# A hybrid block on one core: meetings inside the transformer calls dropped, first steps of what follows put in the last feed-forward rounds, loops written out, 3 and 3 banks

## The chip, the cores and the metric

One core of a Trainium2 chip runs the whole kernel. Its engines are TensorE (PE in the profile: matrix products and transposes, into eight PSUM banks of 128x512 fp32), VectorE (DVE), ScalarE (ACT), GpSimd (POOL) and SyncE (SP, which here only issues DMAs). Each takes its own instructions in order and waits for the others by semaphores. The metric is the device time of one execution in microseconds. Before the change it was 2386.45 us, the median of three runs (2385.03 to 2386.71).

## The reference

Eight sequences of 512 tokens and 128 features go through four steps, each added to a residual and fed with a layer norm of it:

```
x = x + mamba_block(layernorm(x))      # phase m
x = x + transformer(layernorm(x))      # phase t0, call 0
x = x + decayed_attention(layernorm(x))# phase a
x = x + transformer(layernorm(x))      # phase t1, call 1
```

The transformer has DEPTH = 2 layers. A layer shifts half the features by one token, projects to q, k and v (8 heads of 64), normalises and rotates q and k, attends within windows of 64 tokens and the window before, projects out and adds. Then it shifts again, takes a layer norm, goes up to 2 x 341 features, multiplies one half by the exact gelu of the other, goes down to 128 and adds. The decayed attention has 16 heads of 8 over all 512 tokens; its scores are multiplied by exp(-|rate| x distance) before the softmax.

## The kernel before, in words

The work is cut by sequence (B = 8) and by tile of 128 tokens (TPS = 4 a sequence). X holds the residual and Y the normed input, both in SBUF for the whole run. Every engine has its own written order; there is no planner. `run` (line 1996 and on) goes through the phases m, t0, a, t1 on each engine and ends each with `meet` (line 332 and on): the engine drains, adds one to a semaphore, and waits until all five have done so.

**A transformer call** is `transformer_sp`, `_pe`, `_act`, `_dve` and `_pool`. For each layer l it runs eight rounds of attention, then a meeting, then eight rounds of feed-forward, then, except after the last layer, another meeting. With the meeting at the phase's end a call has four. q counts sequences over layers and calls, s within a layer.

*Attention.* Before the first sequence the engines fill a pipeline: SyncE stages the shifted input in yq (`stage_shifted`, L446 to L450), TensorE transposes it (L513), VectorE copies it to hT (L835), TensorE projects tiles 0 and 1 to q, k (L519) and v (L526), ScalarE squares (L708) and copies v (L714), VectorE rotates (L842, L847) and sums squares (L854, L856), GpSimd adds (L1004), takes the root (L1010) and normalises (L1019). `qk_transpose` (L533) and the projections of tile 2 follow. Then `attention_sequence` does, for each tile, scores (a mask product L546 and products L553), maxima (L860), exponentials (L730), transposes of the probabilities (L566), the products with v (L578), the transposes of the outcome (L586), the output projection (L592) and its addition (L878), with the preparation of later tiles in between. GpSimd builds the rope tables of the layer first (L1040, L1044), after the wait for the attention weights.

*Feed-forward.* SyncE stages the shifted Y of each sequence in one of two buffers fq (`stage_ff`, L459 to L461); it waits for the sequence's last output addition and until the buffer's last user has been normalised. Sequences 0 and 1 are staged before the meeting and 2 to 7 after it, then come the loads of the next attention weights (`load_attn`, L423 to L426). VectorE takes statistics (`ff_stats`, L912, L917), GpSimd the inverse root (`ff_rstd`, L1055, L1057), VectorE normalises (`ff_normalize`, L925). TensorE transposes (`ff_normed`, L626) and ScalarE scales to fnT (L767). In `ff_round`, TensorE goes up in three steps i of two products each (`ff_up`, L638, into banks 3 to 6 by turns), ScalarE takes the gelu of one (L762), VectorE multiplies (`ff_product`, L933), and TensorE goes down for the sequence before (`ff_down`, L647, bank 7 or 0), which VectorE adds (`ff_add`, L943). TensorE's order in a round is up 0, transposes of sequence q+1, up 1, down of q-1, up 2. VectorE's is product 2 of q-1, statistics of q+2, product 0, normalisation of q+2, product 1, addition of q-1. In a last layer GpSimd adds Y to X (`pre_add`, L1049), and in call 0 VectorE and GpSimd also take the layer norm of sequences 0 and 1 for the decayed attention there (`norm_stats`, `norm_rstd`, `norm_apply`).

*Decayed attention.* `x_transpose` (L1141) and `project` (L1149) make q and k, ScalarE adds the bias (`with_bias`, L1268, L1269), GpSimd splits the result in three bf16 parts (`split`, L1390 to L1397), SyncE writes them to DRAM (`send`, L1111) and reads them back in nine combinations, a half of the heads at a time (`combine`, L1107). Then, per head: four score products (L1165) into banks 0 and 1 by turns, VectorE scales them and takes their maxima (L1319), GpSimd subtracts (L1403), TensorE transposes in four turns (`turn`, L1174) into banks 2 to 5, ScalarE takes the exponential (L1276) and TensorE multiplies with v (`weigh`, L1185) into bank 6. Bank 7 serves the projections.

Most of the sequences are rounds of a loop on each engine (`Fori`, a counter in a register and a jump back); the first and the last one or two of a phase are written out.

`credits` gives semaphores a start value, so that a wait for "n uses ago" is a plain wait for a count. For the banks of the decayed attention these are:

```python
(scaled_done, 2), (aexp_done, TPS)
```

## Time and profile before

| | |
|---|---|
| runs (3) | 2386.45 us median, 2385.03 to 2386.71 |
| the profiled execution | 2385.01 us |
| its span, first to last instruction | 2383.2 us |
| instructions in the profile | 60302 |
| TensorE busy | 2184.3 us (92%) |
| VectorE busy | 1627.2 us (68%) |
| ScalarE busy | 1489.7 us (63%) |
| GpSimd busy | 1679.1 us (70%) |
| granted TensorE clock, mean | 0.97 of full speed |
| SyncE's DMA queue | 119248 packets, 82.70 MB |
| the two instruction queues | 69 packets, 1.13 MB and 77 packets, 0.63 MB |

A busy share is the time in which the engine had an instruction under way. It is a mean over stages that have little in common, so the stretches are to be read one by one. The stretches are: mamba phase to about 300 us, then call 0 (attention to 593, feed-forward to 671, attention to 963, feed-forward to 1045), the decayed attention (first scores at 1072) to about 1630, then call 1 (attention to 1931, feed-forward to 2010, attention to 2301, feed-forward to the end).

In the rows, a time in brackets is how long the engine had been idle before, with what ended that wait. "DVEq L336" there is the meeting's wait.

### The profile page before, as it was taken

To read this page: it belongs to the slowest core of one execution; us is meant where nothing else is said; L and a number is where in the kernel's file an instruction comes from. 1 tells how busy PE (TensorE), PEld (TensorE's weight loads), DVE (VectorE), ACT (ScalarE), POOL (GpSimd) and SP (SyncE) were. 2 spreads that over 40 slices of the span, in tenths; PEclk is the share of its full clock that TensorE was granted. 3 is DMA by queue.
4 is the path that set the end of the run, shared out by engine and by line. 5 is a ranking of instruction groups with operands and counts; after the bars stand their busy time and mean duration, and the time that the engine had idled before them with its cause. 6 is when DMAs were issued, how large, how long until landed. Compare 5 with 4: busy or idle time off the path is not lost. (4 is left out here: it accounts for less than half of the span.)

```text
span 2383.2 us, 60302 instructions
## 1 busy us (share of the span) xinstructions
PE 2184.3 (92%) x19744; PEld 1490.5 (63%) x19760; DVE 1627.2 (68%) x3905; ACT 1489.7 (63%) x4130; POOL 1679.1 (70%) x1712
## 2 busy tenths in 40 slices
PE   6998789998989999859999999998999978999979
PEld 4766557776557777535655656564777755677755
DVE  5777578886557777537666667675878745777755
ACT  3556368887358887325655556554888843888853
POOL 5777788886168888228777777766889822888842
PEclk8999899999999999889999999998999999999999
DMA  4000011111111111112111111101111112111101
GB/s 111 1 0 1 6 27 34 40 37 30 48 36 36 36 34 33 27 58 58 54 42 34 52 53 37 49 21 25 28 34 40 43 23 51 36 34 36 39 21 50
DMA packets 121250, 86.69 MB, mean 36 GB/s; under 512 B 85560, under 2 KB 102160, under 8 KB 118800
## 3 DMA queue, kind: packets, MB, share of 16 engines
q1 hardware_dynamic: 119248, 82.70, 14.3%
q10 hardware_dynamic: 1856, 2.23, 0.3%
q8 instruction: 69, 1.13, 0.2%
q14 instruction: 77, 0.63, 0.1%
HBM read 30.38 MB, written 8.39 MB: 16 GB/s over the span
## 5 line engine op out<-in xcount | busy, mean ns | idle before, releaser
L1319 DVE CUSTOM_DVE_ANT_0 store<-bank,store 128x512 f32<-128x512 f32 x512 | 340.1, 689 | 170.2 <-PE bank L1165 108.6
L1403 POOL TENSOR_SCALAR store<-store 128x512 f32<-128x512 f32 x512 | 349.7, 694 | 149.5 <-DVE store L1319 147.4
L1276 ACT ACTIVATE store<-bank 128x512 f32<-128x512 f32 x512 | 287.1, 603 | 251.2 <-PE bank L1174 247.7
L730 ACT ACTIVATE store<-bank,store 128x128 f32<-128x128 f32 x1024 | 364.2, 378 | 68.5 <-DVE store L860 68.4
L1010 POOL TENSOR_TENSOR store<-store 128x16 f32<-128x16 f32 x128 | 372.5, 2910 | 26.6 <-DVE store L856 26.6
L1004 POOL TENSOR_TENSOR store<-store 128x512 f32<-128x512 f32 x256 | 321.0, 1275 | 85.0 <-DVE store L847 83.7
L1174 PEld LDWEIGHTS bank<-store 128*128 128x128 f32 x2048 | 241.4, 142 | 130.4 <-ACT store L1276 74.1
L1174 PE MATMUL bank<-store 128*128 128x128 f32 x2048 | 298.3, 278 | 0.0
L519 PE MATMUL bank<-store 128*128 128x512 f32 x512 | 270.1, 615 | 7.1 <-DVE store L835 6.6
L1019 POOL TENSOR_TENSOR store<-store 128x512 f32<-128x512 f32 x256 | 261.5, 1043 | 17.4 <-POOL store L1010 11.4
L860 DVE TENSOR_REDUCE store<-bank 128x4 f32<-128x512 f32 x256 | 165.0, 686 | 130.4 <-PE bank L553 130.4
L736 ACT ACTIVATE store<-bank 128x512 f32<-128x512 f32 x256 | 157.8, 616 | 114.0 <-PE bank L566 114.0
L730 ACT ACTIVATION_READ_ACCUMULATOR store<-bank,store 128x1 f32 x1024 | 222.1, 217 | 0.0
L1165 PE MATMUL bank<-store 72*128 72x512 bf16 x512 | 183.2, 389 | 39.5 <-DMA store<-parts 22.0
L638 PE MATMUL bank<-store 128*128 128x512 f32 (+1 forms) x384 | 189.4, 630 | 27.8 <-DVE store L933 22.8
L533 PEld LDWEIGHTS bank<-store 128*128 128x128 f32 x1024 | 116.3, 141 | 129.1 <-POOL store L1019 103.2
L533 PE MATMUL bank<-store 128*128 128x128 f32 x1024 | 154.8, 281 | 35.1 <-POOL store L1019 33.1
L842 DVE TENSOR_TENSOR store<-bank,store 128x512 f32<-128x512 f32 x256 | 174.5, 682 | 12.9 <-issue 6.2
L847 DVE TENSOR_TENSOR store<-bank,store 128x512 f32<-128x512 f32 x256 | 174.4, 681 | 0.0
L592 PEld LDWEIGHTS bank<-store 128*128 128x128 f32 x1024 | 133.5, 192 | 63.8 <-ACT store L741 38.7
L762 ACT ACTIVATE store<-bank,store 128x512 f32<-128x512 f32 (+1 forms) x96 | 65.9, 686 | 170.7 <-PE bank L638 168.4
L566 PEld LDWEIGHTS bank<-store 128*128 128x128 f32 x1024 | 120.8, 141 | 75.9 <-issue 68.1
(199 smaller groups left out, 4457.3 us busy)
## 6 DMA issues: line engine op xcount, KB each, us to landing
store<-store SPq DMA_DIRECT2D x256, 128.0 KB, 2.3
store<-parts SPq DMA_DIRECT2D x96, 192.0 KB
parts<-store SPq DMA_DIRECT2D x16, 384.0 KB, 3.6
store<-store SPq DMA_DIRECT2D x128, 32.0 KB
store<-store SPq DMA_DIRECT2D x128, 31.8 KB
store<-store SPq DMA_DIRECT2D x32, 127.0 KB
store<-in_L_ffn_wqkv_dram SPq DMA_DIRECT2D x4, 768.0 KB, 4.6
out_dram<-store SPq DMA_DIRECT2D x8, 256.0 KB, 2.5
```

Source lines behind the costliest of these rows:

```text
L519: nc.tensor.matmul(bank[i][:, :], hT[:, j * P:(j + 1) * P], wqkv[:, i * INNER:(i + 1) * INNER], start=True, stop=True).then_inc(qk_done, 1)
L533: last = nc.tensor.transpose(bank[5 + i][:, b * P:(b + 1) * P], roped[:, i, b * P:(b + 1) * P], ident)
L638: nc.tensor.matmul(to, w1[:, half * HID + at:half * HID + at + n], fnT[:, odd, :], start=True, stop=True).then_inc(up_done, 1)
L730: last = nc.scalar.activation(prob[:, e, b, :], bank[3 + e][:, b * P:(b + 1) * P], ACT.Exp, bias=nmax[:, e, b:b + 1], accum_out=psums[:, h ...
L1004: nc.gpsimd.tensor_tensor(straight[:, at, :], straight[:, at, :], turned[:, at, :], ALU.add).then_inc(add_done, 1)
L1010: nc.gpsimd.tensor_tensor(flat, flat, minus_half[:, 0:2 * H], ALU.pow).then_inc(norm_done, 1)
L1019: nc.gpsimd.tensor_tensor(roped[:, i, :].rearrange("p (h d) -> p h d", d=DH), straight[:, at, :].rearrange("p (h d) -> p h d", d=DH), bc(n ...
L1165: nc.tensor.matmul(bank[t % 2][:, :], QC[0:COMBO, h, t * P:(t + 1) * P], KC[0:COMBO, h, :], start=True, stop=True).then_inc(score_done, 1)
L1174: last = nc.tensor.transpose(bank[2 + c][:, t * P:(t + 1) * P], S[:, h % 4, t, c * P:(c + 1) * P], ident)
L1276: nc.scalar.activation(AT[:, h % 4, c, :], bank[2 + c][:, :], ACT.Exp, scale=-1.0).then_inc(aexp_done, 1)
L1319: nc.vector.tensor_tensor_reduce(out=S[:, h % 4, t, :], in0=bank[t % 2][:, :], in1=decay[:, off:off + L], scale=1.0, scalar=-3.0e38, op0=A ...
L1403: nc.gpsimd.tensor_scalar(s_, s_, -1.0, amax[:, h % 4, t:t + 1], ALU.mult, ALU.add).then_inc(shifted_done, 1)
```

## The change

It has five parts.

1. **The meetings inside a call go.** Only the one at each phase's end stays. Waits on single semaphores take their place: TensorE waits for the last v copy before it transposes for feed-forward in bank 2, for the last exponentials before it goes up into banks 3 and 4, for the last copy of the probabilities before banks 5 and 6, for the last output addition before bank 7 is used, and for all feed-forward additions before the next layer's scores. Feed-forward's transposes and its up steps 0 and 1 of the first sequence are put between the last steps of attention. SyncE stages sequences 2 to 7 right after the last v shifts; the loads of the next attention weights stand behind the staging of sequence 3, and those of the second layer's feed-forward weights inside its attention, before the last staged sequence.
2. **The next layer's fill is put in the last rounds of feed-forward.** The four input transposes (now bank 1) in round 6, the projections of tile 0 in round 7, those of tile 1 around the last down (now bank 3), then the q, k transposes of tile 0 and the projections of tile 2. VectorE, ScalarE and GpSimd have their parts at the matching places.
3. **The decayed attention's first steps are put in call 0's last feed-forward.** Layer norm of sequences 0 and 1 in rounds 3 and 5, transposes and first projection in round 4, second projection in round 5 (all in bank 1), the splits after GpSimd's last pre-addition, sending and combining at the end of SyncE's part of the call.
4. **All loops are written out**, in every phase: `with pe.Fori(1, B - 1) as s` becomes `for s in range(1, B - 1)`.
5. **The decayed attention's banks** are 3 for the scores (0 to 2) and 3 for the turns (3 to 5), by a running count, in place of 2 and 4.

The diff, cut to its core:

```diff
+        SCORE_BANKS, TURN_BANKS = 3, 3
-                   (scaled_done, 2), (aexp_done, TPS), (at_done, 16), (ao_ready, 1), (av_out, TPS),
+                   (scaled_done, SCORE_BANKS), (aexp_done, TURN_BANKS), (at_done, 16), (ao_ready, 1), (av_out, TPS),
...
         def transformer_sp
-                if l:
-                    sp.wait_ge(down_added, q0 - B + 2)
-                    for j in range(TPS):
-                        stage_shifted(sp, 0, q0, j)
-                    meet(sp, 2 * l + meets)
-                    load_ff(sp, l)
-                with sp.Fori(0, B - 1) as s:
+                for s in range(0, B - 1):
                     if l == 0:
                         sp.wait_ge(ln_ready, B * norm + s + 2)
+                    else:
+                        sp.wait_ge(down_added, q0 - B + s + 3)
+                        if s == B - 2:
+                            load_ff(sp, l)
...
-                meet(sp, 2 * l + meets + 1)
                 for s in range(2, B):
                     stage_ff(sp, s, q0 + s)
-                if call == 0 or l == 0:
-                    load_attn(sp, 1 - l)
+                    if s == 3 and (call == 0 or l == 0):
+                        sp.wait_ge(wo_done, 4 * (q0 + B))
+                        sp.wait_ge(tab_ready, 6 * (l + (call * DEPTH + 1)))
+                        load_attn(sp, 1 - l)
+                if l < DEPTH - 1:
+                    sp.wait_ge(down_added, q0 + 2)
+                    for j in range(TPS):
+                        stage_shifted(sp, 0, q0 + B, j)
...
         def transformer_pe
+            def ff_rounds(q0, l):
+                new = l < DEPTH - 1
+                q1 = q0 + B
+                for s in range(B):
+                    q, odd = q0 + s, s % 2
+                    if s:
+                        ff_up(q, 0, odd)
+                    if new and s == B - 1:
+                        pe.wait_ge(attn_w, (l + 1 + (call * DEPTH + 1)) * (16 * ATTN_LOADS))
+                        pe.wait_ge(down_added, q0 + B - 1)
+                        begin_qk(q1, 0)
+                    if call == 0 and not new and s == 4:
+                        decayed_x(pe)
+                    if s < B - 1:
+                        ff_normed(q + 1)
+                    if s:
+                        ff_up(q, 1, odd)
+                    if new and s == B - 2:
+                        begin_x(q1)
+                    if new and s == B - 1:
+                        project_v(q1, 0, False)
+                    if call == 0 and not new and s == 5:
+                        decayed_project(pe, 1)
+                    if s:
+                        ff_down(q - 1, 1 - odd, bank[7 if odd else 0])
+                    ff_up(q, 2, odd)
+                    if call == 0 and not new and s == 4:
+                        decayed_project(pe, 0)
+                if new:
+                    begin_qk(q1, 1)
+                ff_down(q0 + (B - 1), 1, bank[3])
+                if new:
+                    project_v(q1, 1, False)
+                    qk_transpose(q1, 0)
+                    for i in range(2):
+                        project_qk(q1, 2, i)
...
-                with pe.Fori(1, B - 1) as s:
+                for s in range(1, B - 1):
                     attention_sequence(q0 + s, True, True)
                 attention_sequence(q0 + (B - 1), True, False)
+                ff_normed(q0, True)
                 weigh_values(q0 + (B - 1), TPS - 1)
+                pe.wait_ge(ff_w, (l + (call * DEPTH + 1)) * (16 * FF_LOADS))
+                ff_up(q0, 0, 0, True)
                 o_transpose(q0 + (B - 1), TPS - 1)
+                ff_up(q0, 1, 0, True)
                 project_out(q0 + (B - 1), TPS - 1)
-                meet(pe, l * 2 + meets + 1)
...
+                pe.wait_ge(wo_added, 4 * (q0 + B) + 1)
+                ff_rounds(q0, l)
...
         def transformer_act
+                    ff_gate(q, 0, odd)
+                    if new and s == B - 1:
+                        squares(q1, 0)
+                    if call == 0 and not new and s == 4:
+                        decayed_copy_xT(act)
+                    if s < B - 1:
+                        ff_affine(q + 1, 1 - odd)
+                    ff_gate(q, 1, odd)
+                    if new and s == B - 1:
+                        copy_v(q1, 0)
+                    if call == 0 and not new and s == 5:
+                        decayed_with_bias(act, 0)
+                    ff_gate(q, 2, odd)
+                    if call == 0 and not new and s == 5:
+                        decayed_with_bias(act, 1)
...
         def transformer_dve
+                    if s:
+                        ff_product(q - 1, 2, 1 - odd)
+                    if decayed and s == 3:
+                        dve.wait_ge(down_added, q0 + 3)
+                        norm_stats(dve, n, 0, 0, FIRST)
+                    if s < B - 2 and s:
+                        ff_stats(q + 2, odd)
+                    ff_product(q, 0, odd)
+                    if new and s == B - 1:
+                        dve.wait_ge(tab_ready, 6 * (l + 1 + (call * DEPTH + 1)))
+                        rotate_tile(q1, 0)
+                    if s < B - 2:
+                        if s == 0:
+                            ff_stats(q + 2, odd)
+                        ff_normalize(q + 2, odd)
+                    if decayed and s in (3, 5):
+                        norm_apply(dve, n, s // 2 - 1, 4 * (s // 2 - 1))
+                    ff_product(q, 1, odd)
+                    if new and s == B - 1:
+                        square_sums(q1, 0)
+                    if s:
+                        ff_add(s - 1, q - 1, bank[7 if odd else 0], not new)
+                    if new and s == B - 2:
+                        for j in range(TPS):
+                            take_x(q1, j, True)
+                ff_product(q0 + (B - 1), 2, 1)
+                if new:
+                    rotate_tile(q1, 1)
+                    square_sums(q1, 1)
+                ff_add(B - 1, q0 + (B - 1), bank[3], not new)
...
         def transformer_pool
+                if l:
+                    pool.wait_ge(rot_done, 8 * q0 + 2)
                 pool.wait_ge(attn_w, (l + (call * DEPTH + 1)) * (16 * ATTN_LOADS))
                 rope_tables()
...
                 if call == 0 and last_layer:
+                    for t in range(2):
+                        decayed_split(pool, t)
...
         def decayed_pe
-                nc.tensor.matmul(bank[t % 2][:, :], QC[0:COMBO, h, t * P:(t + 1) * P], KC[0:COMBO, h, :],
+                nc.tensor.matmul(bank[(64 * q + k) % SCORE_BANKS][:, :], QC[0:COMBO, h, t * P:(t + 1) * P], KC[0:COMBO, h, :],
...
-            x_transpose(0, True)
-            project(0, 0)
-            project(0, 1)
...
-            with pe.Fori(1, B - 1) as q:
+            for q in range(1, B - 1):
                 sequence(q, True, True)
```

## Rows read from the trace of the kernel before

**Rows 1.** Windows: stretch, us, busy PE, PEld, DVE, ACT, POOL; clock, DMA

```profile
593.00:671.00 78.00, 70.40 (x320) 42.80 (x320) 37.29 (x108) 28.43 (x37) 7.59 (x12) 0.96 0.16 38
...
1045.00:1072.00 27.00, 2.87 (x9) 0.97 (x10) 0.48 (x1) 4.41 (x6) 6.62 (x7) 0.65 0.28 82
...
1072.00:1630.00 558.00, 540.28 (x3912) 331.71 (x3912) 386.31 (x1197) 321.82 (x586) 413.32 (x583) 0.99 0.16 43
```

**Rows 2.** Timeline, SyncE, first feed-forward: start us, us, line, operation

```profile
594.62 6.52 SPq L461 DMA_DIRECT2D store<-store  x1
...
635.47 6.53 SPq L461 DMA_DIRECT2D store<-store  x1
```

**Rows 3.** Timeline, VectorE, first statistics after the meeting

```profile
603.26 0.87 DVE L912 BATCH_NORM_STATS2 store<-store 128x6 f32<-128x128 f32 x4 [8.27 <-DMA store<-store]
```

**Rows 4.** Timeline, TensorE, first feed-forward and the next layer's start

```profile
587.90 1.44 PE L578 MATMUL bank<-store 128*64 128x64 f32 x32
...
591.48 1.16 PE L592 MATMUL bank<-store 128*128 128x128 f32 x8 [0.69 <-ACT store L741]
...
610.54 0.60 PE L626 MATMUL bank<-store 128*128 128x128 f32 x4
...
651.88 0.60 PE L626 MATMUL bank<-store 128*128 128x128 f32 x4
...
652.31 1.88 PE L638 MATMUL bank<-store 128*128 128x512 f32 x4
...
654.03 2.84 PE L647 MATMUL bank<-store 128*128 128x128 f32 x24
...
656.71 5.31 PE L638 MATMUL bank<-store 128*85 128x512 f32 x12
...
687.95 0.41 PE L546 MATMUL bank<-store 64*64 64x512 bf16 x4
```

**Rows 5.** Timeline, TensorE and SyncE, from call 0 to the decayed attention

```profile
1041.13 2.92 PE L647 MATMUL bank<-store 128*128 128x128 f32 x24 [1.00 <-DVE store L933]
...
1071.93 1.03 PE L1165 MATMUL bank<-store 72*128 72x512 bf16 x2 [22.03 <-DMA store<-parts]
...
1052.14 0.39 SPq L1111 DMA_DIRECT2D parts<-store  x1
```

**Rows 6.** Timeline, VectorE and TensorE, decayed attention, starts of sequences

```profile
1276.63 0.69 DVE L1319 CUSTOM_DVE_ANT_0 store<-bank,store 128x512 f32<-128x512 f32 x1 [2.56 <-PE bank L1174]
...
1346.86 0.69 DVE L1319 CUSTOM_DVE_ANT_0 store<-bank,store 128x512 f32<-128x512 f32 x1 [2.75 <-PE bank L1174]
...
1486.16 0.69 DVE L1319 CUSTOM_DVE_ANT_0 store<-bank,store 128x512 f32<-128x512 f32 x1
...
1553.81 0.69 DVE L1319 CUSTOM_DVE_ANT_0 store<-bank,store 128x512 f32<-128x512 f32 x1
...
1277.39 0.39 PE L1165 MATMUL bank<-store 72*128 72x512 bf16 x1 [1.56 <-DVE store L1319]
```

**Rows 7.** Timeline, TensorE, the same two places in the second layer

```profile
960.67 1.90 PE L592 MATMUL bank<-store 128*128 128x128 f32 x8 [0.69 <-ACT store L741]
...
982.13 0.60 PE L626 MATMUL bank<-store 128*128 128x128 f32 x4
```

**Rows 8.** Timeline, VectorE, a normalisation in the last feed-forward

```profile
2354.58 3.99 DVE L925 TENSOR_SCALAR store<-store 128x128 f32<-128x128 f32 x4 [0.90 <-POOL store L1057]
```

**Rows 9.** Timeline, GpSimd, root and normalisation, written out and in the loop

```profile
555.61 2.91 POOL L1010 TENSOR_TENSOR store<-store 128x16 f32<-128x16 f32 x1 [0.21 <-DVE store L856]
...
558.60 2.04 POOL L1019 TENSOR_TENSOR store<-store 128x512 f32<-128x512 f32 x2
...
2084.30 2.91 POOL L1010 TENSOR_TENSOR store<-store 128x16 f32<-128x16 f32 x1 [0.21 <-DVE store L856]
...
2087.43 2.04 POOL L1019 TENSOR_TENSOR store<-store 128x512 f32<-128x512 f32 x2 [0.22 <-POOL store L1010]
```

**Rows 10.** Waits over the span: us in total, times, longest

```profile
PE bank L1165 <- DVE store L1319: 17.2, 39, 1.7
```

More of the change, by code:

```diff
@@ new lines, in decayed_split, with decayed_combine @@
+        def decayed_split(pool, t):
+            for step in range(3):
+                split_step(pool, 0, t, step)
+        def decayed_combine(sp, t, half):
+            heads = slice(half * HA // 2, (half + 1) * HA // 2)
+            to = (QC, KC)[t]
+            parts = parts_dram[t].rearrange("a (d h) n -> a d (h n)", d=DA)[:, :, half * HALF:(half + 1) * HALF]
+            for x in range(PARTS):
+                rows = to[x * PARTS * DA:(x + 1) * PARTS * DA, heads, :].rearrange("r h n -> r (h n)")
+                sp.dma_start(rows, bc(parts[x], 0, PARTS) if t == 0 else parts).then_inc(combos_in[half], 16)
@@ L1119, in decayed_sp @@
             load_ff(sp, 0)
-            with sp.Fori(0, B - 1) as q:
+            for q in range(0, B - 1):
                 for half in range(2):
@@ L1365, in decayed_dve @@
             sequence(0, False, True, True)
[L1366 removed]
+            for q in range(1, B - 2):
                 sequence(q, True, True, True)
@@ L1418, in sequence @@
                         for step in range(3):
-                            split(q + 1, h // 2 - 3, step)
-            for t in range(2):
-                for step in range(3):
-                    split(0, t, step)
-            with pool.Fori(0, B - 2) as q:
+                            split_step(pool, q + 1, h // 2 - 3, step)
+            for q in range(0, B - 2):
                 sequence(q, True, True)
```

348 lines of the change are left out of this document (155 added, 193 removed).

## The prediction

> **What bounds the kernel now.** I read the busy time by stretch first, then the chain of waits of each stretch, then its timeline engine by engine. No single engine bounds the 2383.2 us. In the feed-forward of one layer TensorE is busy 70.4 of 78 us; in the 27 us between the first transformer call and the decayed attention it is busy 2.9 us; in the decayed attention it is busy 540 of 558 us [rows 1]. So time can be won only where TensorE starts late, and four kinds of place show that.
>
> First, feed-forward starts. SyncE stages the shifted copy of sequences 2 to 7 only after the meeting. Each takes 8.17 us of SyncE's queue, 6.5 us of it the third of its three issues, and all six go out back to back [rows 2]. VectorE takes its work in order, so it waits 8.27 us for the first copy [rows 3], and TensorE in turn for VectorE. After that TensorE never stops: from 610.54 to 651.88 five rounds take 41.3 us, 8.27 each, against 8.17 for SyncE. A round is one transpose group (0.44 us), three up pairs (1.72 each) and one down (2.68), by the starts of the rows from 651.88 on [rows 4]. So the pace is TensorE's, and the late start is what is lost.
>
> Second, the next layer's start: from the last transpose group at 651.88 to the first scores at 687.95 go 36.1 us [rows 4], most of the last 18 of them a fill with little work. Third, the decayed attention's start: last down at 1041.13, ending 1044.05, first score at 1071.93, with 22.03 us of TensorE waiting for the parts' trip through DRAM; SyncE sent the first part at 1052.14 [rows 5]. Fourth, the loops: in the decayed attention VectorE stands 2.56 to 2.75 us wherever its loop jumps back, and TensorE 1.56 us; where the code is written out (1486.16) no idle time is put to it [rows 6].
>
> **Part 1, feed-forward starts (four).** TensorE's new order, counted from the end of the last probability transposes at 587.90, which is 3.6 us before the old output projection at 591.48: transposes 0.5, value products 1.44, up 0 1.72, transposes 0.6, up 1 1.72, output projection 1.2 (7.2 so far); VectorE's addition 0.3 and product 0.7, statistics and aggregation 1.2, GpSimd's root 1.3, normalisation 1.1, product 0.7, up 1.72: 14.3, so the transposes of sequence 2 stand 10.8 us behind the mark. Before it was 19.1 us (591.48 to 610.54) [rows 4], 21.5 us in the second layer (960.67 to 982.13) [rows 7] and 19.3 us in each layer of the second call. In the first the decay table's two instructions on ScalarE (2.0 us) stay ahead of the first gate: 12.8. Gains: 6.3 + 10.7 + 8.5 + 8.5 = 34.0. The meeting's drain is in this. What must hold: stage 2 can be issued when VectorE has normalised sequence 0 (about 582), 11 us earlier; stage 3 at about 591.5. The four loads of the next attention weights now stand behind stage 3 on SyncE, 2.0 us; stage 7 then lands near 636 instead of 644, and TensorE at 8.27 a round needs it by about 640. Cover about 3 us; in round 2 it is under 1 us. Bounds: 4 x 6 = 24 if a round or so slips, 40 if the cold clock of the second layer goes too.
>
> **Part 2, next layer's start (two).** From the transpose group of sequence 7: 0.44, up 1.72, four x transposes 0.6, down 2.68, up 1.72; round 7: up 1.72, two projections 1.72, up 1.72, value projection 0.86, down 2.68, up 1.72, two projections 1.72, last down 2.68, value projection 0.86, two transpose groups 1.2, two projections 1.72, copy 0.7: 26.5. Before 36.1; the second call has 36.3. Gains 9.6 + 9.8 = 19.4. All these steps ran before too; they move from an idle stretch into a busy one, so their TensorE time is counted in full. GpSimd's rope tables and first finishing steps fall in its idle rounds. VectorE takes 2 rotations and a sum (4 us) in round 7, where it has 5 us to spare. SyncE's shifted copies of the next sequence 0 need only the addition of sequence 0, long done. The new wait of the first scores for the last addition costs up to 1 us. Bounds: 12 to 24 for both.
>
> **Part 3, the decayed attention's start.** Old gap 1044.05 to 1071.93, 27.9 us. New: addition and meeting 1.5. TensorE pays in the rounds for four transposes and two projections (0.44 + 2 x 0.86) and about 1.5 of waiting: the second projection stands behind ScalarE's two copies, themselves behind a gate; down and the last up are queued behind it. That is 3.7. Gain 27.9 - 1.5 - 3.7 = 22.7. The layer statistics moved from round 6 to 3 stop TensorE up to 2 us, about as they did. The first part should be ready near 1015 and the trip takes 19.8 us (1052.14 to 1071.93) [rows 5]: 1035, with the last addition near 1038. Cover 3 us. GpSimd's six split steps (1.0 each) lie beside VectorE's work. What speaks against is contention: four normalisations of VectorE took 3.99 us, about 1 us being usual, while GpSimd added [rows 8]. The Trainium skill, "GPSIMD Engine Reference", section 1, says that GpSimd shares its SBUF interfaces with VectorE, against instructions in a two-port mode or with two SBUF inputs. By it each moved normalisation that meets a split would cost about 3 us more. I take none, since most land beside ScalarE's copies, and keep 2 x 3. Bounds: 14 to 25.
>
> **Part 4, loops.** Decayed attention: a looped sequence takes 70.2 us (1276.63 to 1346.86), a written-out one 67.6 (1486.16 to the next at 1553.8, no layer norm in it). Four back edges at 1.56 (TensorE's own gap) to 2.6: 6 to 10, taken 9 because VectorE's gap is nearer the upper end [rows 6]. Attention: in GpSimd's looped part the normalisation of every second tile stands 0.22 us behind the root before it, in the written-out last tiles none [rows 9] (by the starts 0.08). The chain of waits goes through this step. 0.14 x 56 tiles = 7.8; bounds 0 and 10. Here no back edge shows a stop. Mamba phase: taken 0, bounds 0 and 2, by the same row. The Trainium skill, "Runtime: NRT & Kernel Launch", section "Instruction fetch mechanics", says a taken branch outside the current window forces a fetch. By it every long body's edge would stop an engine; the decayed rows agree, the attention's show none.
>
> **Part 5, banks.** A third score bank lets TensorE run further ahead of VectorE: TensorE waited for it 17.2 us in all, edges included [rows 10]. The fourth turning bank goes: turning (0.6), 0.4 of hand-over, exponential 0.6, return 0.2 make 1.8 us, against three turns at 0.66 = 2.0, so it just holds except where ScalarE has other copies. I take +3, bounds -4 and +8.
>
> **Sum.** 34.0 + 19.4 + 22.7 + 9 + 7.8 + 3 = 95.9. The profiled execution took 2385.01 (span 2383.2): 2289.1. The median of the runs is 1.4 above it: 2290.5, say 2291.
>
> **Rivals.** (a) Feed-forward turns bound by SyncE and VectorE's order: stage loads at 8.17 a sequence with 2.0 of weights between, statistics ahead of products. For: the cover in round 2 is under 1 us. Against: 8.17 is below 8.27. If six rounds of four stages lose 2 us each: 48 less, 2339. (b) The moved steps save little because TensorE is full there: parts 2 and 3 keep only half, 21 less, 2312. For: 70.4 of 78 busy. Against: the fills they leave are nearly empty. (c) Slower: straight-line code is fetched too slowly. Each of the 48 bodies that were loop rounds (8 mamba, 32 attention, 8 decayed) would stop once for the 2.56 us seen at an edge: 123 us, 2414; it decides from 38 stops on. Against: first and last sequences are written out already, and their tiles run at the same pace. The same section of the skill says that crossing a block in straight code is mostly hidden; by it (c) gives nothing. (d) The change does not do what it says: waits kept in another form (the projection's wait for all attention weights, the scores' for the last addition) leave parts 2 and 3 where they were: 42 less, 2333.
>
> **Numbers.** Forecast 0.72, (a) 0.10, (b) 0.10, (c) 0.04, (d) 0.04. The bounds of the parts add up to gains of 52 and 119, 2334 and 2267; all ends together are unlikely, and (b) and part of (a) are taken in: 2270 to 2330. A measurement of this kernel can tell about 0.2%, 5 us. Faster 0.95, same 0.01, slower 0.04.
>
> **What would show it.** Right: no VectorE wait near 8 us before the first statistics; transposes of sequence 2 about 11 us behind the output projection; 26 to 27 us from the transposes of sequence 7 to the first scores; under 3 us from the last down of the first call to the first score; decayed sequences of 67 to 69 us without a gap where loops closed; no 0.22 before the normalisation. Wrong: rounds above 8.5 us, a wait for the parts that is still above 5 us, or idle gaps of 2 us in written-out code. The forecast fails if feed-forward rounds slow down by what the start wins.

## The result, and the profile after

The changed kernel takes **2282.82 us** (median of 4 runs, 2282.32 to 2289.8), against 2386.58 (2385.03 to 2388.57) for the kernel before on the same chip: a ratio of 0.957, 95% interval 0.955 to 0.959. That is 103.8 us less; the prediction had 2291 us, which is 95.9 less. The profiled execution's span went from 2383.2 to 2280.7 us. The page's first lines, and its line on the instruction queues:

```profile
span 2280.7 us, 54552 instructions
## 1 busy us (share of the span) xinstructions
PE 2155.9 (95%) x19760; PEld 1486.3 (65%) x19760; DVE 1617.2 (71%) x3905; ACT 1477.0 (65%) x4122; POOL 1680.1 (74%) x1712
...
q8 instruction: 159, 2.61, 0.5%
...
q14 instruction: 108, 0.88, 0.1%
```

TensorE has the products of before and stands idle 125 us of the span instead of 199. Where the time came from, by the starts of TensorE's rows in both traces (us; the last column is what the forecast put there):

| stretch | gain | forecast |
|---|---|---|
| start to first attention scores | 0.9 | 0 |
| attention, first to last scores (4 stages) | 4.0 | 7.8 |
| last scores to the transposes of sequence 2 (4) | 6.8 + 9.4 + 7.4 + 6.1 = 29.7 | 34.0 |
| transposes of sequence 7 to the next layer's scores (2) | 10.7 + 11.0 = 21.7 | 19.4 |
| transposes of sequence 2 to the first decayed score | 20.9 | 22.7 |
| decayed attention to the next call's first scores | 24.9 | 9 + 3 |
| rest | 0.5 | 0 |

Before rounding the pieces add up to 102.5, the difference of the spans. The rounds keep about 8.27 us in three of four feed-forwards; in the one ahead of the decayed attention, where part 3 put its steps, they lose time (the row that starts at "transposes of sequence 2 to the first decayed score" has that loss in it). The rows of TensorE that answer to [rows 4] and [rows 5], and the second layer of the second call (timeline of the changed kernel; start, duration, wait before it in brackets):

```profile
643.43 0.60 PE L634 MATMUL bank<-store 128*128 128x128 f32 x4
...
668.77 0.41 PE L552 MATMUL bank<-store 64*64 64x512 bf16 x4
...
1016.88 2.92 PE L658 MATMUL bank<-store 128*128 128x128 f32 x24 [1.00 <-DVE store L987]
1020.63 0.82 PE L1259 MATMUL bank<-store 72*128 72x512 bf16 x3 [0.83 <-DVEq L337]
...
2213.43 3.65 PE L650 MATMUL bank<-store 128*128 128x512 f32 x4 [3.74 <-DVE store L987]
2216.91 0.60 PE L634 MATMUL bank<-store 128*128 128x128 f32 x4
```

The reader is to see three things. From sequence 7's transposes to the scores go 25.3 us instead of 36.1. The first decayed score stands 0.83 us behind the meeting instead of 22.03 us behind a transfer. And a new wait of 3.74 us for VectorE's product (L987) stands in the feed-forward's start: part 1 falls short there.

### The profile page after: what moved, and what is told of

Read it like the earlier page. It is cut to its first block and busy times, and to the rows that moved or that the text cites. A ratio compares the mean times of both kernels' runs of the same rounds, so it can differ in the third digit from the quotient of the medians.

```text
span 2280.7 us, 54552 instructions
## 1 busy us (share of the span) xinstructions
PE 2155.9 (95%) x19760; PEld 1486.3 (65%) x19760; DVE 1617.2 (71%) x3905; ACT 1477.0 (65%) x4122; POOL 1680.1 (74%) x1712
## 5 line engine op out<-in xcount | busy, mean ns | idle before, releaser
L1407 DVE CUSTOM_DVE_ANT_0 store<-bank,store 128x512 f32<-128x512 f32 x512 | 335.5, 689 | 119.0 <-PE bank L1259 66.8
L1070 POOL TENSOR_TENSOR store<-store 128x16 f32<-128x16 f32 x128 | 372.8, 2912 | 28.2 <-DVE store L910 28.2
L650 PE MATMUL bank<-store 128*128 128x512 f32 (+1 forms) x384 | 184.2, 612 | 16.6 <-DVE store L987 16.6
L1259 PE MATMUL bank<-store 72*128 72x512 bf16 x512 | 175.9, 383 | 3.7 <-DVE store L1407 2.5
```

What stands on the lines that cost most here:

```text
L650: nc.tensor.matmul(to, w1[:, half * HID + at:half * HID + at + n], fnT[:, odd, :], start=True, stop=True).then_inc(up_done, 1)
L1070: nc.gpsimd.tensor_tensor(flat, flat, minus_half[:, 0:2 * H], ALU.pow).then_inc(norm_done, 1)
L1407: nc.vector.tensor_tensor_reduce(out=S[:, h % 4, t, :], in0=bank[(64 * q + 4 * h + t) % SCORE_BANKS][:, :], in1=decay[:, off:off + L], sca ...
```

## The experiments

Two things limit what small differences can say. The kernel before was timed again beside each group of runs, with medians of 2384.29 to 2387.05 us, so a few us between runs of different groups may be the group's. And the first attention scores, ahead of which no edit below changes anything, start between 314.7 and 320.6 us in the traces of the changed kernel and its variants; why was not looked for. What an edit did is therefore read from the pieces of the trace behind that point. In each experiment "A", "B", "C", "P" and "Q" are the theories of the expectation above it.

**e1_banks24.** One size undone:

```diff
-        SCORE_BANKS, TURN_BANKS = 3, 3
+        SCORE_BANKS, TURN_BANKS = 2, 4
```

> The changed kernel with one thing undone: the decayed attention has its 2 score banks and 4 turn banks back (it is still written out). The decayed attention gained 24.5 us, 3.5 a sequence, where the forecast had 12 (9 for its loops' stops, 3 for the bank). Theory A, the third score bank: a score no longer waits for the exponential two steps back, and this gives the 15 us that the stops at the loops' ends leave: about 2298 to 2303 us, each sequence about 2.5 us longer than 66.6. Rival B, the written-out code: the forecast's 3 us for the bank was right and the code without loops gives the rest: about 2286 us, each sequence about 0.4 us longer.

2295.67 us (ratio 0.9615, 0.9586 to 0.9645), 12.9 slower than the changed kernel. Theory A, though its reason is misnamed: by the code a score product waits until VectorE has scaled the score that had its bank, not for the exponential. It shows in the windows of one sequence (us, then busy PE, PEld, DVE, ACT, POOL), the changed kernel first:

```profile
1213.45:1280.08 66.63, 66.55 (x495) 41.60 (x493) 48.06 (x151) 40.67 (x75) 52.59 (x74) 1.00 0.17 49
```

and with 2 and 4 banks:

```profile
1219.13:1287.47 68.34, 67.25 (x494) 41.43 (x494) 48.54 (x151) 40.81 (x75) 52.50 (x74) 1.00 0.17 47
```

The changed kernel's TensorE is idle for only 0.08 us here. With two banks it idles 1.1 us and is busy 0.7 us more with the same work. Whether a fourth score bank would add anything was not run: as the next rows show, a TensorE that counts as busy can still hide a loss. In the groups of the two pages, the score products with 3 banks and then with 2:

```profile
L1259 PE MATMUL bank<-store 72*128 72x512 bf16 x512 | 175.9, 383 | 3.7 <-DVE store L1407 2.5
```

```profile
L1259 PE MATMUL bank<-store 72*128 72x512 bf16 x512 | 181.7, 385 | 12.1 <-DVE store L1407 11.1
```

They differ by 8.6 us of waiting for VectorE and 5.8 us of busy time: 14.4 of the 15.0 us by which the decayed attention is longer (572.6 against 557.6). The second part is not a wait in the profile.

**e3_banks23.** `SCORE_BANKS, TURN_BANKS = 2, 3`.

> The changed kernel with 2 score banks and 3 turn banks in the decayed attention, so one bank is left idle. It parts what the third score bank gives from what the fourth turn bank was worth. The waits at the turn banks in the profile of before (39 of them, 17.2 us of idle time in all) were waits for the one before the last store, and a fourth bank did not shorten them. Theory A: the third turn bank costs nothing by itself, the score bank is all: within 1 us of the run with 2 and 4 banks. Rival: the turn banks matter as well and lose 3 to 8 us here, so that the third score bank gives correspondingly more than the run with 2 and 4 banks shows.

2296.77 us (0.9619, 0.959 to 0.9648); against e1's 2295.67; spans 2294.1 and 2293.9. Theory A: beside two score banks the fourth turning bank was worth nothing that these runs can tell. (The 39 waits and 17.2 us that the expectation gives to the turning banks are those of the score products [rows 10].)

**e2_loops_a.** Banks 2 and 4, and the decayed attention's loops restored:

```diff
-            for q in range(1, B - 1):
+            with pe.Fori(1, B - 1) as q:
```

and so on SyncE, ScalarE, VectorE and GpSimd.

> The changed kernel with 2 and 4 banks and the loops of the decayed attention restored on all five queues, so that this phase is the one of before. The decayed attention should take its 24.5 us back: about 2307 us. Against the run with 2 and 4 banks written out it prices the loops alone. Theory A (the stops of VectorE at the loop's end, 1.6 to 1.9 us a turn, and little else): 9 to 10 us. Rival B (the code without loops gives most of the gain): 20 us or more.

2296.3 us (0.9606, 0.9576 to 0.9636), no different from e1. **Both theories fell.** The phase has the loops and banks of before again and takes 571.5 us, where before it took 582.5. No stop of VectorE at the loop's end is over 0.2 us. Something other than the loop had cost 11 us. A difference stands in the transfers by queue over about three turns (q14 fetches instructions): the kernel before

```profile
q1 hardware_dynamic: 3433, 8.78, 15.3%
q14 instruction: 12, 0.10, 0.2%
```

and this run over about the same turns, with no row for an instruction queue:

```profile
q1 hardware_dynamic: 3677, 10.34, 16.3%
```

Before, five blocks of 8192 bytes come in every turn. By VectorE's records, three of them start when it has executed instruction 1603, 1730 and 1855 of its program (with loops counted once), about 128 apart; the others are at the jump back, two of them beside VectorE's stop. Its loop's body, 1567 to 1863, lies across four such blocks if the blocks go on at that spacing; in e2 (2153 to 2449) across three. That is so far a reading of two traces, and f1 puts it to the test.

**f1_before_shift.** The kernel *before*, with VectorE's loop moved along its program:

```diff
             nc.vector.memset(bank[6][:, :], 0.0)
+            for _ in range(110):
+                dve.wait_ge(ln_ready, 1)
             sequence(0, False, True, True)
```

> The kernel before, with 110 waits that are met already (55 instructions, two waits in each) added on VectorE ahead of the decayed attention, where it waits over 15 us anyway; nothing else is changed and every loop stays. Putting the decayed loops back into the changed kernel cost nothing (2296.3 against 2295.7 us), and there the trace shows no instruction transfer in the turns, where the kernel before has 5 blocks of 8 KB in every turn, one of them in VectorE's stop of 2 to 2.75 us at the loop's end. Counting VectorE's executed instructions, the loop's 297 lie over 4 blocks of 128 in the kernel before and over 3 in the changed one. Theory P, it is the place of the loop in VectorE's program: moved by 55 instructions the loop lies over 3 blocks, the instruction transfers of the turns and the stops go, about 1.8 us a turn for five turns: 8 to 11 us faster than the kernel before, about 2377 us. Rival Q, the stops belong to the loop and its length and something else in the changed kernel removed them: same as before, 2386 to 2388 us, the stops stay.

2377.25 us (9 runs) against 2384.29 (11 runs): ratio 0.9963, 0.9952 to 0.9974. That is 7 us by the medians and 9 by the ratio, for 55 instructions that do nothing. Theory P. VectorE at the loop's end, which answers to the 2.56 of [rows 6] (the loop's first scaling is the last row):

```profile
1283.11 0.69 DVE L1319 CUSTOM_DVE_ANT_0 store<-bank,store 128x512 f32<-128x512 f32 x1
1283.72 0.08 DVE L1319 DVE_READ_ACCUMULATOR2_ANT store<- 128x1 f32 x1
1283.90 0.69 DVE L1319 CUSTOM_DVE_ANT_0 store<-bank,store 128x512 f32<-128x512 f32 x1
```

By the starts of TensorE's scores the turns that had a stop are 1.8, 1.8, 2.0 and 3.6 us shorter, the phase takes 572.9 us, and from 1220 to 1420 us there is no instruction transfer. The loop and its length are the same, so what had cost the time was its place. Only this one other place was tried. (The profiled execution lost 11 us before the first attention; the timed ones did not.)

**e4_pool_loop.** GpSimd's attention loops restored, with two forms for l = 0 and 1 as before:

```diff
-                for s in range(B):
-                    attention_sequence(s, q0 + s, s < B - 1, l == 0 and s < B - 2)
...
+                    with pool.Fori(0, B - 1) as s:
+                        attention_sequence(s, q0 + s, True)
...
```

> The changed kernel with GpSimd's loop over the sequences of the four attention stages restored, the other engines written out. In the profile of before GpSimd's second softmax step came 0.22 us after the first instead of 0.08 us inside the loop. Forecast was 7.8 us for this, the stages gained 4.0 us. Theory A (the gap is GpSimd's own register arithmetic and is passed on at half its size, since only one in two of the steps ends last): 3 to 4.5 us, about 2286.5 us. Rival B (the gap is passed on in full): 7 to 8 us, about 2290.5 us. Rival C (GpSimd's gap hides and the loops of the other engines gave the gain): under 1 us.

2291.12 us (0.959, 0.9562 to 0.9618): 8.3 slower, nearest to B by its total. GpSimd's gap of [rows 9] is back:

```profile
1644.18 2.91 POOL L1070 TENSOR_TENSOR store<-store 128x16 f32<-128x16 f32 x1 [0.21 <-DVE store L910]
1647.31 2.04 POOL L1079 TENSOR_TENSOR store<-store 128x512 f32<-128x512 f32 x2 [0.22 <-POOL store L1070]
```

But only 4.4 us lie in the attention stages, as theory A had it. Of the 10.0 us by which the span is longer, the other 5.6 are lost ahead of the first attention (0.8), in the feed-forwards (4.1) and in the decayed attention (0.7). Why these take longer with a loop on GpSimd was not tried.

**e5_att_loops.** The same, and the loops of TensorE, ScalarE and VectorE.

> The changed kernel with the loops over the sequences of the attention restored on GpSimd, TensorE, ScalarE and VectorE; the run with GpSimd's alone was 8.3 us slower than the changed kernel (4.4 of it in the attention stages of the trace). Theory A (the other engines' loops stop nowhere: their bodies of 95 to 136 instructions lie over few blocks): the same as with GpSimd's loop alone, 2290 to 2292 us. Rival B (three more loops have a price at every turn): 2294 to 2300 us.

2292.83 us (0.9602, 0.9587 to 0.9617), span 2291.1 against e4's 2290.7. Theory A, a little above its range: these loops cost 0.4 us by the spans and under 2 by the medians, which is within the noise.

**e6_part3_off.** `decayed_x`, `decayed_project`, the copy and biases, `decayed_split` and `decayed_begin_sp` taken out of the rounds and put first in the decayed attention's functions:

```diff
-                    if kind == "sp" and call == 0:
-                        decayed_begin_sp(eng)
...
         def decayed_sp(sp):
+            decayed_begin_sp(sp)
```

> The changed kernel with the decayed attention's first steps (transpose of x, both projections, copy and bias, splits, the first two sends and combines) put back behind the feed-forward and the meeting; the order of the normalisations is left as changed. Theory A (the forecast's step: 22.7 us gained between the last down projection and the first decayed score, with the trace showing 27.1 for the gap and 6 given back in the rounds): 20 to 23 us slower than the changed kernel, about 2304 us, and TensorE waits some 22 us again before the first decayed score. Rival B (the chain of splits and combines overlaps other work anyway, since the meeting no longer comes first on each queue): under 15 us.

2310.2 us (0.9682, 0.966 to 0.9703), 27.4 slower; the span is 28.2 longer, of which 4.9 lie ahead of the first attention, which the edit does not touch. From there: 26.8 in the gap, less 3.1 that the rounds take back, 23.6. Theory A by these pieces; the total is above its 20 to 23. TensorE:

```profile
1026.75 2.07 PE L1151 MATMUL bank<-store 128*128 128x512 f32 x2 [1.36 <-ACT store L1160]
1049.62 2.77 PE L1245 MATMUL bank<-store 72*128 72x512 bf16 x5 [20.80 <-DMA store<-parts]
```

It also halves the loss of the rounds: of the 6.15 us that they lose in the changed kernel, 3.1 belong to the moved steps. The other 3.0 are left by subtraction; e6 keeps the earlier normalisation, and with it TensorE's wait of 2.86 us for the product behind it, as in the changed kernel.

**e7_part2_off.** `if new and s == B - 1:` and the like made false in TensorE's, ScalarE's and VectorE's rounds, and the fill before the first sequence done in both layers, as before.

> The changed kernel with the next layer's first steps (transposes, projections, rotations and first scores of sequences 0 and 1 in the last rounds) put back behind the feed-forward, in both calls. Theory A (the steps are what TensorE lacked after the last down projection): the trace's gain from the last transpose of the feed-forward to the first scores, 10.7 and 11.0 us in the two calls, goes: about 20 to 22 us slower, 2303 to 2305 us. Rival B (part of it was the meeting between the layers, which this run does without too): 10 to 15 us slower, 2293 to 2298 us.

2305.42 us (0.9668, 0.9643 to 0.9693), 22.6 slower. Theory A: of its 23.1 us in the span 21.4 lie where the trace of the changed kernel has its 21.7 of gain, so nothing of it was the meeting's.

**e8_meet.** One meeting ahead of each feed-forward, on all engines:

```diff
+                meet(pe, 0)
                 pe.wait_ge(wo_added, 4 * (q0 + B) + 1)
                 ff_rounds(q0, l)
```

> The changed kernel with one meeting of all engines put back between the attention and the feed-forward of each layer (4 in all), everything else as changed. The gain of 29.7 us in the trace from the last scores to the third transpose of the feed-forward is either the meeting's or that of the first steps placed ahead of it. Theory A (the meeting alone: the feed-forward's transposes for sequences 0 and 1 stay ahead, so only what waits for the last addition of the attention comes late): 3 to 5 us at each of the four places, 12 to 20 us slower, about 2299 us. Rival B (the meeting is nearly free, because TensorE waits for the last output's addition anyway): 0 to 4 us. Rival C (the whole 29.7 us): about 2312 us.

2326.16 us (0.9751, 0.973 to 0.9772): 43.3 slower, over all three theories. The meeting alone costs more than part 1 had won. SyncE, VectorE and TensorE of this run:

```profile
596.75 0.64 SPq L463 DMA_DIRECT2D store<-store  x1
...
604.87 0.66 SPq L463 DMA_DIRECT2D store<-store  x1
```

```profile
606.89 0.87 DVE L972 BATCH_NORM_STATS2 store<-store 128x6 f32<-128x128 f32 x4 [5.29 <-DMA store<-store]
```

```profile
611.78 3.75 PE L654 MATMUL bank<-store 128*128 128x512 f32 x4 [6.41 <-DVE store L993]
```

Behind the meeting SyncE stages sequence 2 at 596.75, and sequence 3 8.1 us later; in the changed kernel it staged sequence 2 at 580.50, and VectorE took the statistics at 595.42 instead of 606.89. This run is 3.55 us late before the meeting already (its first attention scores start at 319.0 against 315.4), so the staging comes 12.7 us later and the statistics 7.9. At the transposes of sequence 2 the delay is 9.6 to 10.7 us in each of the four feed-forwards, 40.3 together: that is what the meetings cost in the trace, of 44.5 us in the span. Most of it is the staging that waits behind the meeting. While TensorE waits its clock falls too: in the 18 us from 597 it is busy 7.36 us at a mean granted clock of 0.57, so mostly at the lower level, 1.2 GHz; in the changed kernel, in the same 18 us (from 593.45), 15.13 us at 0.91:

```profile
597.00:615.00 18.00, 7.36 (x12) 2.49 (x11) 4.43 (x15) 6.33 (x8) 1.26 (x2) 0.57 0.17 35
```

**b1_first_product.** VectorE, round 0:

```diff
+                    if s == 0:
+                        ff_stats(q + 2, odd)
+                        ff_product(q, 1, odd)
                     if s < B - 2:
-                        if s == 0:
-                            ff_stats(q + 2, odd)
                         ff_normalize(q + 2, odd)
...
-                    ff_product(q, 1, odd)
+                    if s:
+                        ff_product(q, 1, odd)
```

> The changed kernel with one step of VectorE moved: in round 0 of each feed-forward the second gated product comes ahead of the normalisation of the third sequence, behind its statistics. In the changed kernel's trace TensorE waits for that product at all four starts (1.72 and 1.15, 3.74, 2.80 and 3.74 us, 13.2 us together), and VectorE is held meanwhile by a wait for GpSimd of 1.58 us and by four normalisations. Theory A (the order on VectorE is what these starts wait for): 10 to 13 us faster than the changed kernel, 2270 to 2273 us. Rival B (the third sequence's normalisation, 0.7 us later now, becomes the next wait): 3 to 6 us faster, about 2278 us.

2280.82 us (0.9556, 0.9536 to 0.9577): 2 us, less than either theory and within the noise (1.7 by the spans). The 3.74 us became 0.37 and the four starts won 12.5 us at the third transposes, but the rounds behind them lost 10.3. VectorE and SyncE in the first layer of the second call:

```profile
1874.84 0.87 DVE L966 BATCH_NORM_STATS2 store<-store 128x6 f32<-128x128 f32 x4 [4.68 <-DMA store<-store]
```

```profile
1864.57 0.72 SPq L461 DMA_DIRECT2D store<-store  x1
1865.33 7.37 SPq L462 DMA_DIRECT2D store<-store  x1
1872.82 0.65 SPq L460 DMA_DIRECT2D store<-store  x1
```

The next wait is the staged copy. SyncE is busy 8 to 9 us with a sequence, nearly all of it in the third copy, which moves 0.8 KB.

**b2_norm_order.** b1, and in the rounds ahead of the decayed attention:

```diff
-                    if decayed and s in (3, 5):
-                        norm_apply(dve, n, s // 2 - 1, 4 * (s // 2 - 1))
                     if s:
                         ff_product(q, 1, odd)
+                    if decayed and s in (3, 5):
+                        norm_apply(dve, n, s // 2 - 1, 4 * (s // 2 - 1))
```

with GpSimd's first `decayed_split` ahead of its `pre_add` of the last three sequences, and the second ahead of the last two.

> The last one, and in the feed-forward ahead of the decayed attention two things more: VectorE normalises the decayed attention's input behind the second product of rounds 3 and 5 instead of ahead of it, and GpSimd's first split comes ahead of its additions for the last three sequences. In the changed kernel's trace TensorE waits 2.86, 1.08, 0.36 and 1.00 us in these rounds, 5.3 us, where the rounds of the other call show none. Theory A (these waits are the norm's place on VectorE): 2 to 4 us faster than the last one, about 2268 us. Rival B (the splits slow VectorE through the port that they share, wherever they stand; the four normalisations beside them took 4.85 us): no change, or up to 2 us slower, as the projections come late instead.

2274.82 us (0.9531, 0.9511 to 0.955), 6.0 faster than b1. Theory A: TensorE's 2.88 us became 0.16, and the rounds ahead of the decayed attention take 4.2 us less. The first decayed score comes 6.3 us earlier, 1.5 of it from ahead of the first attention. The run moved the normalisation and the splits together, so what each gave was not parted; the wait that went is the normalisation's.

**b3_split_copy.** b2, and SyncE's second copy in two:

```diff
-            sp.dma_start(fq[1:P, odd, :, 64:P], y[0:P - 1, :, 64:P]).then_inc(f_in[odd], 16)
+            sp.dma_start(fq[1:113, odd, :, 64:P], y[0:112, :, 64:P]).then_inc(f_in[odd], 16)
+            sp.dma_start(fq[113:P, odd, :, 64:P], y[112:P - 1, :, 64:P]).then_inc(f_in[odd], 16)
```

> The last version (both orders moved) with SyncE's second copy of the feed-forward's staging split in two, rows 1 to 112 and rows 113 to 127. What the earlier first product gained at the third transpose (12.5 us over four starts) was given back by the next sequences, whose statistics on VectorE wait 1.4 to 4.7 us for the staged copies: SyncE is busy 8.0 to 8.1 us with a sequence, 6.5 of them in the small third copy, which is held while the 508 rows of the second trickle in at 18 GB/s. Theory A (127 rows go through one DMA engine, where 128 go through all of them; 112 rows spread as well): the third copy takes under 1 us of SyncE, its chain is short, and the give-back goes: 4 to 8 us faster than the last version, 2267 to 2271 us. Rival B (the trickle is a limit of the queue, not of the row count): no change, within 1.5 us. Rival C (the copies are soon enough, and the give-back is TensorE's own pace): SyncE's time per sequence falls but the time stays.

**2268.8 us** (0.9497, 0.9484 to 0.951), 6.0 faster than b2 and 14 faster than the changed kernel: the best version of the study. Theory A. In the trace the rounds of the four feed-forwards, from the third transposes to the eighth, take 9.2 us less than b2's, most of what b1's rounds had given back (the profiled execution lost 5.8 us ahead of the first attention). SyncE's issues for one sequence in b3, and the last of b2's:

```profile
2211.25 0.68 SPq L460 DMA_DIRECT2D store<-store  x1
2211.97 0.66 SPq L461 DMA_DIRECT2D store<-store  x1
2212.67 0.91 SPq L462 DMA_DIRECT2D store<-store  x1
2213.62 0.73 SPq L463 DMA_DIRECT2D store<-store  x1
```

```profile
2208.73 6.50 SPq L462 DMA_DIRECT2D store<-store  x1
```

3.1 us of SyncE instead of 7.9, one copy more. The transfer rate (GB/s, 15 us in 40 slices, the changed kernel from 2222, then b3 from 2210) shows what held the third copy:

```profile
GB/s 203 157 14 14 14 16 17 18 18 18 18 18 18 18 18 18 18 18 18 19 18 17 0 119 212 27 16 14 15 18 16 62 18 18 18 18 18 18 18 18
```

```profile
GB/s 0 0 0 0 0 0 13 225 140 190 88 41 0 2 0 0 0 0 0 0 0 0 0 0 0 0 152 193 147 156 34 14 2 0 0 44 0 0 0 0
```

The 127 rows trickled at 18 GB/s; 128, 112 and 15 rows don't. From 2224 to 2229 us of the changed kernel, with no other queue at work, the packets fill 7.9% of the time of the core's 16 DMA engines, so as much as 1.3 engines. That fits theory A's single engine; the trace does not name the engine of a packet.

## Why the prediction was right

The forecast said 95.9 us, and the chip gave 103.8 (102.5 in the span). Parts 1, 2 and 3 gained by the mechanisms that the forecast gave, and most of the gain is theirs. That the total came so near is partly luck: the terms that fell short and those that came out larger offset each other. Two readings were wrong, the cause of the stops in part 4 and the size of part 5.

**Part 1** came out at 29.7 for 34.0. The starts are about as worked out up to the transposes of sequence 1 (6.9 us behind the mark in the first feed-forward, 7.2 forecast); then the terms "normalisation 1.1, product 0.7, up 1.72" fail. VectorE of the changed kernel:

```profile
2210.57 2.05 DVE L979 TENSOR_SCALAR store<-store 128x128 f32<-128x128 f32 x4 [1.58 <-POOL store L1117]
2212.54 1.40 DVE L987 SCALAR_TENSOR_TENSOR store<-bank,store 128x512 f32<-128x512 f32 x2
```

In a last layer the four normalisations run beside an addition of GpSimd (from 2210.51 on, 1.26 us) and take 2.05 us; only then comes the product that TensorE needs. It has been idle for 3.74 us by then, and its next four products take 3.65 us, where four take 1.9 elsewhere. The windows of this place (clock before the last two columns):

```profile
2210.00:2213.40 3.40, 0.00 (x0) 0.01 (x1) 2.83 (x6) 0.00 (x0) 1.77 (x2) 1.00 0.08 19
2213.40:2217.00 3.60, 3.57 (x5) 1.49 (x6) 1.70 (x9) 0.69 (x1) 1.48 (x3) 0.53 0.21 46
2217.00:2222.00 5.00, 5.00 (x34) 3.95 (x33) 2.58 (x7) 1.47 (x2) 1.03 (x1) 1.00 0.08 18
```

The stretch behind the idle one runs at the lower level, so the wait is paid twice. The forecast's "up 1.72" did not allow for that. The forecast gave SyncE's cover in round 2 as "under 1 us", and that was the sharpest sentence in it: b1 took 12.5 us off the starts and the rounds gave 10.3 back, and b3, which changes SyncE's copies alone, won 9.2 in the rounds. e8 delayed the same chain by a meeting in each layer and lost 40. Rival (a) had the right mechanism, in a kernel a few us faster than this one.

**Part 2** (21.7 for 19.4) and **part 3** (20.9 for 22.7) hold within 2.3 us each, and e7 and e6 take them away again at their size. In part 3 the gap gave 27.05 for 26.4, and the rounds cost 6.15 for 3.7. The moved steps themselves cost 3.1 (e6), under the 3.7. What went beyond the forecast is the layer statistics and normalisation moved from round 6 to 3, which were to stop TensorE "about as they did": e6 leaves them 3.0, and b2, by putting the normalisation behind a product, takes away the wait. The contention that was priced and then left out is there, at a smaller size. Round 5 in the changed kernel, then in e6, which has the same normalisations and no splits beside them:

```profile
991.60 4.85 DVE L979 TENSOR_SCALAR store<-store 128x128 f32<-128x128 f32 x4 [0.30 <-POOL store L1117]
996.37 2.38 DVE L881 TENSOR_SCALAR store<-store 128x128 f32<-128x128 f32 x4
```

```profile
995.96 3.99 DVE L967 TENSOR_SCALAR store<-store 128x128 f32<-128x128 f32 x4 [0.95 <-POOL store L1105]
999.87 1.11 DVE L869 TENSOR_SCALAR store<-store 128x128 f32<-128x128 f32 x4
```

GpSimd's three additions ran from 991.53 to 995.24 beside the first row, its first split from 995.21 beside the end of it and beside the second. The additions alone account for 3.99 us, in e6 and in the kernel before (2.9 us over the 1.1 of four normalisations by themselves); the split adds 0.86 to the first row and 1.27 to the second, 2.1 us of VectorE's time. So the forecast's "I take none" was too low by that and its 3 us for each normalisation that meets a split too high, and the sum of the moved steps held all the same. The contention fits the rule of the Trainium skill, "GPSIMD Engine Reference", section 1, on the shared SBUF interfaces.

**Part 4**, decayed attention: 9 for the loops' ends, and the runs give 11.0 (e2) and 9.6 (f1), of which 9.3 and 9.4 lie between the first and the last score. The size was right and the name was wrong. It is not the loop that cost it but where its body lay: f1 keeps the loop and loses the stop. Writing it out (e1 against e2) gave nothing more. The Trainium skill, "Runtime: NRT & Kernel Launch", section "Instruction fetch mechanics", has the rule for it (a jump to a target outside the current window waits for a fetch), and these traces agree that a jump back can wait for a fetch. The page's block is 16 KiB and the packets here are of 8192 bytes, so the sizes go by the traces: a body over four blocks of 8192 bytes is fetched again each turn (before), one over three is not (e2, f1). That would also be why the attention's loops show no stop, which the prediction left as a contradiction: VectorE's bodies there have 95 to 117 instructions and can't reach four blocks. Attention: 4.0 for 7.8 in the stages, though GpSimd's loop is worth 8.3 in all.

**Part 5** is the step that was mis-sized: "+3" for the banks, and e1 measures 13 (15 within the phase). The row was there: 17.2 us of waits [rows 10], of which four edges of 1.56 make 6.2. The 11 us that are left stand in the runs with two score banks and no stops (10.5 in f1, 11.1 in e1), and the third bank removes all but 2.5. The forecast set a loss from the fourth turning bank against it, and e3 finds none. Another 5.8 us could be read in no wait in advance: they sat in the scores' busy time.

So the sum was 6.6 us short of the profile's 102.5: -4.3 in part 1, -3.8 in part 4's attention, -1.8 in part 3, +2.3 in part 2, +12.9 in the decayed attention and +1.3 outside the parts. Errors of 9.9 us one way and 16.5 the other left 6.6. **The rivals:** (c) had no new stop of 2 us at straight code, with 108 and 159 instruction blocks (q14 and q8) instead of 77 and 69; (b) and (d) are excluded by e6 and e7.

## What to carry to other kernels

Before an engine is called free in a pipelined round, add up its queue per round, issues included, and write the cover beside the pace: here SyncE's 8.1 against 8.27 us hid a limit that ate most of the next 12.5 us won, and splitting one copy lifted it. Where the engine that waits for a bank is the one that bounds the stage, take the wait row whole as what another bank may give: here it was 11 us and the bank gave 13 to 15. A stop at a loop's end is to be tested by moving the loop, before unrolling it.

## What was not expected of the hardware

- The place of a loop in an engine's program cost 9.6 to 11 us of its phase: 55 instructions that do nothing, put ahead of VectorE's loop, made the kernel before 0.4% faster.
- A copy of 127 partitions between SBUF tiles moved at 18 GB/s and held the next issue on its queue for 6.5 us; as 112 and 15 partitions the queue was free after 0.91 and 0.73 us.
- A semaphore meeting ahead of a feed-forward cost about 10 us each (e8), through the transfers queued behind it and a granted clock of 0.57 in the stretch that follows.
